# Splitting rounds spread over seven attention tiles, mixing sums on VectorE, another order at changes of pair, last down weights in used places

## What is computed

```python
h = layernorm(x) * (1 + ca) + sa
x = x + ga * attn(h)                 # sigma(q) @ memories / norms, mixed over 4 banks, @ Wo.T
h = layernorm(x) * (1 + cb) + sb
g = silu(h @ w_gate) * (h @ w_up)    # 512 -> 2048
x = x + gb * (sparsify_2to4(g) @ w_down)
```

## Time and profile before

| | us |
|---|---|
| median of 3 runs | 1488.85 |
| lowest, highest | 1488.25, 1491.37 |
| the profiled execution | 1491.06 |
| its span, first to last instruction | 1489.3 |
| PE busy | 1368.1 (92%) |
| DVE busy | 927.5 (62%) |
| ACT busy | 575.2 (39%) |
| POOL busy | 848.5 (57%) |
| mean granted clock of PE | 0.962 |

### The profile page before, as it was taken

How to read it: one execution, slowest core, us unless ns; L and a number is a source line. 1 busy time by engine, 2 the same in 40 slices (tenths; PEclk the granted TensorE clock), 3 DMA queues, 4 the chain that set the end, 5 groups by cost and what they waited for, 6 DMA issues and landing times.

```text
span 1489.3 us, 18667 instructions
## 1 busy us (share of the span) xinstructions
PE 1368.1 (92%) x6578; PEld 1105.1 (74%) x6578; DVE 927.5 (62%) x1408; ACT 575.2 (39%) x973; POOL 848.5 (57%) x856
## 2 busy tenths in 40 slices
PE   8999999999988999977988998989999899999976
PEld 4688788777767887756766777867788787888865
DVE  6677777766154555435665565756666567666776
ACT  5467667764322322232332342223343232333231
POOL 1877787787565565547885772266553235342224
PEclk9999999999999999988999999999999999999998
DMA  6656566658794756786867787848576583664512
GB/s 234 199 159 203 183 183 198 212 167 320 240 296 138 240 146 203 249 302 211 281 208 238 233 260 271 317 133 287 191 232 219 186 310 121 235 223 147 182 48 80
DMA packets 198285, 315.95 MB, mean 212 GB/s; under 512 B 12468, under 2 KB 146100, under 8 KB 183740
## 3 DMA queue, kind: packets, MB, share of 16 engines
q1 hardware_dynamic: 173868, 150.31, 32.3%
q0 software_dynamic: 24336, 164.64, 31.9%
HBM read 221.56 MB, written 93.34 MB: 211 GB/s over the span
## 4 chain that ended last, share of the span: by engine, by line
PE 52%; POOL 16%; DMA 10%; issue 8%; DVE 7%; ACT 6%; SPq 2%; POOLq 0%; DVEq 0%; ACTq 0%
PE bank L1561 17%; PE bank L1562 16%; PE bank L1563 16%; POOL hs_lo L694 3%; POOL mix L603 2%; DMA mix<-in_w_gu_dram 2%; DMA mix<-in_w_down_dram 2%; POOL banks_r L646 2%; POOL h_lo L572 2%; DMA mix<-h2T_scratch 1%; SPq L405 1%; POOL y L702 1%; PE bank L1632 1%; PE bank L1570 1%; DVE banks_r L1276 1%
## 5 line engine op out<-in xcount | busy, mean ns | idle before, releaser
L1561 PE MATMUL bank<-acts,ring 128*128 128x512 f32 x928 | 372.1, 401 | 53.7 <-ACT keep_u L984 23.1
L1562 PE MATMUL bank<-acts,ring 128*128 128x512 f32 x928 | 368.8, 397 | 0.0
L1563 PE MATMUL bank<-acts,ring 128*128 128x512 f32 x928 | 368.4, 397 | 0.0
L694 POOL TENSOR_TENSOR hs_lo<-hidden,hs_hi 128x512 fp32r<-128x512 f32 x120 | 163.7, 1380 | 245.2 <-ACT hs_hi L1006 245.2
L1561 PEld LDWEIGHTS bank<-acts,ring 128*128 128x128 f32 x928 | 179.1, 193 | 98.8 <-issue 49.8
L1561 PE MATMUL bank<-wd,hs_hi 128*128 128x512 f32 x480 | 194.5, 405 | 24.7 <-POOL hs_lo L694 17.0
L1563 PEld LDWEIGHTS bank<-acts,ring 128*128 128x128 f32 x928 | 178.9, 193 | 38.4
L1562 PEld LDWEIGHTS bank<-acts,ring 128*128 128x128 f32 x928 | 179.5, 193 | 36.9
L1562 PE MATMUL bank<-wd,hs_hi 128*128 128x512 f32 x480 | 191.2, 398 | 0.0
L1563 PE MATMUL bank<-wd,hs_lo 128*128 128x512 f32 x480 | 190.7, 397 | 0.0
L603 POOL TENSOR_TENSOR mix<-mix,mix_hi 128x512 fp32r<-128x512 f32 (+1 forms) x64 | 101.9, 1606 | 112.9 <-ACT mix_hi L866 112.4
(11 more groups left out here) (153 smaller groups left out, 2599.0 us busy)
## 6 DMA issues: line engine op xcount, KB each, us to landing
ring<-wmix_scratch POOLq DMA_DIRECT2D x48, 1024.0 KB, 7.6
ring<-wmix_scratch POOLq DMA_DIRECT2D x48, 768.0 KB, 5.2
wd<-wd_scratch POOLq DMA_DIRECT2D x16, 2048.0 KB, 9.7
acts<-amix_scratch POOLq DMA_DIRECT2D x25, 1024.0 KB, 8.3
mix<-in_w_gu_dram SPq DMA_DIRECT2D x64, 256.0 KB, 4.1
ring<-wmix_scratch POOLq DMA_DIRECT2D x32, 512.0 KB, 5.1
amix_scratch<-mix_hi SPq DMA_DIRECT2D x24, 448.0 KB, 3.8
amix_scratch<-mix SPq DMA_DIRECT2D x24, 448.0 KB, 5.0
```

What stands on the lines that cost most here:

```text
L694: nc.gpsimd.tensor_tensor(lo, slot_of(side, J * m + j), hi.bitcast(F32), ALU.subtract).then_inc(hs_lo_done, 1)
L1561: nc.tensor.matmul(out_, stat[0], mov[0], start=start, stop=False, skip_group_check=resumed)
L1562: nc.tensor.matmul(out_, stat[0], mov[1], start=False, stop=False, skip_group_check=resumed)
L1563: return nc.tensor.matmul(out_, stat[1], mov[0], start=False, stop=stop, skip_group_check=resumed)
```

## The change

It has these parts.
1. Splitting: seven rounds a tile in tiles 0 to 6, none in tile 7, instead of six in each of eight. All 16 down rounds are in the list; 49 places hold 8 "B", 32 "W" and 9 "D", the last 7 "D" rounds go to the mixing rounds. The seventh round's high part is copied at the start of the next tile.
2. Mixing (`TAKE`): units 0 to 3 of pair 0 take one "W" and one "D" instead of two "A"; units 4 to 11 one "W" and one "A"; 12 and 13 a "W" and a "D"; 14 a "D"; 15 none. Pair 1: two "W" in units 0 to 4 and 6, a "W" and an "A" in 5 and 7 to 11, two "A" in 12. Pair 2 as before, one "A" in units 2 to 9.
3. `mix_comb` moves from GpSimd to VectorE, to the end of each unit's work in `half`.
4. GpSimd: `load_down` first, then hs_low and `mix_low` by turns. ScalarE: the two first `hs_high` of a chunk move behind the second `mix_high`.
5. Unit 15's order becomes P6, P7, P1 of the next, P4, P2 of the next, P3; P5 of the next comes behind the down half. keep3 of unit 15 comes ahead of keep1. Loads of activations for pair 1 begin one unit sooner (unit 13).
6. The last down weights go into `acts` P1 and P2, loaded in unit 15 of pair 3. The last item's side 0 uses P5 and P6, side 1 `hs_hi` and `hs_lo`.

```diff
-        PER_TILE = SPLIT_RING
-        others = weight_rounds(*range(UNITS)) + down_rounds(0, 1)
+        PER_TILE = 7
+        others = weight_rounds(*range(UNITS)) + down_rounds(0, 1, 2, 3)
-        for t in range(NT):
+        for t in range(NT - 1):
-        weights_left, downs_left = weight_rounds(*range(UNITS)), down_rounds(2, 3)
+        weights_left, downs_left = weight_rounds(*range(UNITS)), others
-        TAKE = {0: [(0, 2, 0)] * 4 + [(1, 0, 1)] * 8 + [(2, 0, 0)] * 4,
-                1: [(2, 0, 0)] * 8 + [(0, 2, 0)] * 4,
+        TAKE = {0: [(1, 0, 1)] * 4 + [(1, 1, 0)] * 8 + [(1, 0, 1)] * 2 + [(0, 0, 1)],
+                1: [(2, 0, 0)] * 5 + [(1, 1, 0), (2, 0, 0)] + [(1, 1, 0)] * 5 + [(0, 2, 0)],
...
+            if m < ITEMS - 1 or side == 1:
+                return hs_hi[:, j], hs_lo[:, j]
+            return acts[:, P5, j // KH, j % KH], acts[:, P6, j // KH, j % KH]
+        def down_of(m, j):
             if m < ITEMS - 1:
+                return wd[:, 0, j], wd[:, 1, j]
+            return acts[:, P1, j // KH, j % KH], acts[:, P2, j // KH, j % KH]
...
+            if u == UNITS - 1:
+                return [(u, P6), (u, P7), (u + 1, P1), (u, P4), (u + 1, P2), (u, P3), (u + 1, P5)]
...
+                if m == ITEMS - 1:
+                    pool.wait_ge(p_done[P2], UNITS * (NP - 1))
+                    nc.gpsimd.dma_start(acts[:, P1:P2 + 1].rearrange("p a b c d -> p (a b c d)").rearrange(
+                        "p (i j d) -> p i j d", i=2, j=J), wd_dram[CHUNKS - 1].bitcast(F32R)).then_inc(wd_in, 16)
+                    return
...
-                for r in before(n):
-                    mix_low(r)
                 if m >= 0 and j == 0:
                     load_down(m)
-                if m >= 0:
-                    hs_low(m, cp, side, 2 * jj)
-                    hs_low(m, cp, side, 2 * jj + 1)
+                rounds = before(n)
+                for i in range(2):
+                    if m >= 0:
+                        hs_low(m, cp, side, 2 * jj + i)
+                    for r in rounds[i:i + 1]:
+                        mix_low(r)
                 for block_ in FINISH.get(u, ()) if p else ():
                     finish(p - 1, block_)
-                for r in AT_STEP[n]:
-                    mix_comb(r)
...
             def hs_high(m, c, side, j, first=False):
-                if m == ITEMS - 1:
-                    act.wait_ge(p_done[(P1, P5)[side]], UNITS * (NP - 1))
+                if m == ITEMS - 1 and side == 0:
+                    act.wait_ge(p_done[P5], UNITS * (NP - 1))
                 elif j == 0 and not first:
                     act.wait_ge(down_done, 2 * S * m + S * side)
...
+            def mix_comb(r):
+                e, kind, at = [mix[r % MIX_RING][:, i] for i in range(OPS + 1)], ROUNDS[r][0], 4 * COMBINED[r]
+                if kind == "D":
+                    return
+                dve.wait_ge(mix_in[r % MIX_RING], LOADED[r])
+                if kind == "W":
+                    nc.vector.tensor_tensor(e[4], e[3], e[2], ALU.add).then_inc(mix_step, 1)
...
                         hidden_b(p, u)
+                        combine(u)
                         up_of_b(p, u + 1)
                         if not (end and side):
                             gate_a(p, u + 2)
                         hidden_a(p, u + 1)
                         gate_b(p, u + 1)
                         hidden_b(p, u + 1)
+                        combine(u + 1)
...
+                if 0 < p < NP - 1:
+                    product(p, UNITS, P5)
```

More of the change, by code:

```diff
@@ L467, in _ @@
             for t in range(NT):
-                ra = PER_TILE * t
+                ra, last = PER_TILE * t, t == NT - 1
                 if t > 0:
+                    split_store_low(ra - 2)
+                    split_store_high(ra - 1)
                     split_store_low(ra - 1)
-                for r in range(ra, ra + 3):
-                    split_store_high(r)
+                if not last:
+                    for r in range(ra, ra + 3):
+                        split_store_high(r)
                 if t > 0:
                     store_x1(t - 1)
-                split_store_low(ra)
-                split_store_low(ra + 1)
+                if not last:
+                    split_store_low(ra)
+                    split_store_low(ra + 1)
                 if t > 0 and t + 2 < NT:
@@ L480, in _ @@
                     sp.dma_start(xr[place(t + 2)][:], x_t[t + 2]).then_inc(x_in[place(t + 2)], 16)
-                for r in range(ra + 3, ra + 6):
-                    split_store_high(r)
+                if not last:
+                    for r in range(ra + 3, ra + 6):
+                        split_store_high(r)
                 if t > 0:
                     store_h2(t - 1)
-                for r in range(ra + 2, ra + 5):
-                    split_store_low(r)
-            split_store_low(len(SPLITS) - 1)
+                if not last:
+                    for r in range(ra + 2, ra + 5):
+                        split_store_low(r)
             stored(sp, len(SPLITS) - 1)
@@ L652, in tile @@
                                             ALU.add).then_inc(comb_done, 1)
-                    if s == 1:
+                    if s == 1 and not last:
                         split_low(ra)
@@ L747, in pair @@
                     items_and_rounds(p, u)
+                    if last and u == UNITS - 1:
+                        load_down(ITEMS - 1)
                     for unit, o in unit_steps(u, last):
@@ L764, in _ @@
             m = ITEMS - 1
-            load_down(m)
             for side in range(SIDES):
@@ L913, in tile @@
                             ln_sqrt(t + 1, 0)
+                        if not first:
+                            split_hi(ra - 1)
+                        if not last:
                             normalize(t + 1, 0, xn1, xn1_done)
@@ L918, in tile @@
                         transposed()
-                        for r in range(ra, ra + 3):
-                            split_hi(r)
+                        if not last:
+                            for r in range(ra, ra + 3):
+                                split_hi(r)
                         if not first:
@@ L1028, in item_work, with first_splits @@
                     hs_high(mp, cp, 1, 3)
+            def first_splits(m, c):
+                if m == 0:
+                    act.wait_ge(x1_out, 16 * NT)
+                hs_high(m, c, 0, 0, first=m == 0)
+                hs_high(m, c, 0, 1)
             def plain_pair():
@@ L1829, in step @@
             def step(p, u):
-                for unit, o in unit_steps(u, p == NP - 1):
+                for unit, o in unit_steps(u, p == NP - 1)[:OPS if u < UNITS - 1 else OPS - 1]:
                     product(p, unit, o)
```

76 lines of the change are left out of this document (39 added, 37 removed).

## The result

| | before | changed |
|---|---|---|
| median, us | 1489.65 (1488.25 to 1491.37) | 1613.87 (1612.60 to 1614.95) |
| ratio | 1 | 1.0833 (1.0814 to 1.0852) |
| profiled execution: time, span, us | 1491.06, 1489.3 | 1612.79, 1611.0 |
| mean granted clock | 0.962 | 0.938 |

A forecast was written before the change was run, and what follows sets the result against it. The prediction took the kernel as bound by TensorE, with some 130 us of waits as the prize. Its terms, -106 + 54 + 70 + 6 + 3 = +27 us on the span of 1489.3, led to 1516 us, range 1458 to 1548.

The forecast's parts named there:

- Ring weights in pair 0: Pair 0: TensorE's ring waits and their clock go, as sums leave GpSimd and activation rounds leave units 0 to 3: -12.4 us.
- hs_lo in pair 0: Pair 0: waits for low halves of hidden values go, as GpSimd's new order puts them ahead of mix_low: -9.6 us.
- Change 0-1: Between pairs 0 and 1: the 10.2 us gap and 4.3 us lost in the next 102 matmuls go: -14.7 us.
- Changes 1-2 and 2-3: At these pair changes, P1 moved back one product shortens the wait for activations: -2.8 us each.
- Pair 1 and 2, all old losses gone: Pairs 1 and 2: old losses, such as keep3 and hs_lo waiting behind mixing, all go: -47.2 and -16.1 us.
- VectorE held in pairs 0 and 1: Down halves: sums waiting for late loads hold VectorE's y additions: +54 us in pair 0, +70 in pair 1.
- Landing at 8 to 10 us into the half: Odd steps: the second round's load lands then, giving TensorE gaps of 6 to 9 us plus 2.6 of clock.
- Pair 2, +6: Pair 2: one round a step, loads two steps ahead, so sums on VectorE cost 4 x 1.4 = 6 us.
- Last down weights: Kernel's end: their wait goes but the end is no shorter; four hs_low follow one by one: +3 us.
- Spread of the splits: Tiles with seven rounds instead of six: GpSimd's added mix_low falls in idle time: 0 us; without that cover 9.
- the first (loads keep up): Rival: lows and loads run near their floors, gaps stay 3 to 5.6 us, kernel faster, mid 1468; chance 0.27.
- The third, the shared ports: Rival: VectorE and GpSimd obstruct each other, a round of sums takes 2.6 us, not 1.1: 1531; chance 0.10.

The follow-up runs named there:

- e1: The changed kernel with the four sums of a mixing round back on GpSimd, last in each step's GpSimd work: 1487.68 us, 0.9984 of the kernel before.
- e14: The changed kernel with ring loads of units from the third on cut to 8 of 128 partitions: 1549.90 us, 1.0404 of the kernel before.
- e13: The changed kernel with both mix_low of a step ahead of both hs_low on GpSimd again: 1538.63 us, 1.0338 of the kernel before.
- e8: e1 with the last item's down weights and high and low halves in their old places: 1483.02 us, 0.9954 of the kernel before.
- e4: The changed kernel with every mix load from the fourth on cut to 8 of 128 partitions: 1601.46 us, 1.0761 of the kernel before.
- e2: The kernel before with only the sums moved to VectorE, at the changed kernel's places in its order: 1537.78 us, ratio 1.0312.
- e17: The changed kernel, sums on VectorE behind the third y addition, mix loads ahead of stores, old last-down-weight places, both mix_low ahead of both hs_low: 1463.83 us.

## Why the prediction was right in direction and wrong in size

The sum gave +27 us on the span and the measured difference is +122. Of the 95 us between them, 37 lie in pair 1, 29 in pair 0, 17 in pair 2, 5 in the change 0-1. Two steps of the prediction failed. One took the old waits for hs_lo and keep_u as gone, though both operands still come through mix_high and the sums (points 2 and 5). The other was the time at which the odd step's load lands, 8 to 10 us into the half (points 6 and 7). What held TensorE, VectorE's queue behind its loads, was right.

1. **Ring weights in pair 0, -12.4**: right. TensorE waits 0.2 us for the ring instead of 10.0, and the first down half starts at 433.2 instead of 445.8.
2. **hs_lo in pair 0, -9.6**: wrong, in sign. The step that failed is "the new order on GpSimd puts them ahead of mix_low". hs_low waits for ScalarE's hs_high, and that stands behind the mix_high of the step's second round, which now waits for VectorE's sums (ScalarE waited 143.5 us for them: 79.6 for L1402, 63.9 for L1409). TensorE waited some 24 us for hs_lo in pair 0, where it had waited 5.1. Being early in GpSimd's order doesn't help an operation whose operand is late; it only makes mix_low later.
3. **Change 0-1, -14.7** (its terms, 10.2 and 4.3, make 14.5): -9.9. The gap of 10.2 went, but activation loads and their clock left 4.8 us of loss in the 102 products.
4. **Changes 1-2 and 2-3, -2.8 each**: the gaps came as computed (0.8 and 2.3 to 2.5), the clock behind them cost 2.1 us, not the 1 that I gave it; pair 3's stage gained 0.5.
5. **Pair 1 and 2, all old losses gone, -47.2 and -16.1**: wrong. keep3 still stands behind mix_high and mix_high behind the sums, only on another engine: keep_u 19.8 us instead of 23.1. In pair 2, 7.8 us of keep_u stayed of 8.9, the waits for y came on top, and the stage grew by 4.1 where I had -12.9. The same holds for e1, which keeps 34.3 us of keep_u and is worth 2 us as a whole.
6. **VectorE held in pairs 0 and 1, 54 + 70**: the mechanism right, the size not. The halves of pair 0 that I priced took 31.7, 32.5, 28.6 and 30.5 us instead of 10.88, together 79.7 over, and the next one 4.7: my 54 is 30 too little. Each has a y gap of 8.7 to 9.6, at the upper end of what I gave, but also 3.3 to 7.2 of hs_lo, which I had put down as gone and then as "1 to 5 later", and half-speed clock twice. In pair 1, steps and halves are 107.8 over full speed, against my 70: y 54.2, up_b 17.5, keep_u 11.0, the rest clock.
7. **Landing at 8 to 10 us into the half**: too early. It was 16 to 21 in the four halves of pair 0, and 6.5 to 13.1 in pair 1. I took the median of weight loads, 4.0, issued by SP into other traffic; but the changed order ties the activation load to the instant at which GpSimd issues its ring loads (1.75 MB in pair 1). In pair 0 the chain also starts later. The fourth of its halves begins at 591.22:

```profile
593.39 0.29 DVE L1404 TENSOR_TENSOR mix<-mix 128x128 f32<-128x128 f32 x1 [6.99 <-DMA mix<-h2T_scratch]
596.42 0.62 ACT L1011 ACTIVATE hs_hi<-hidden 128x512 fp32r<-128x512 f32 x1
602.55 3.02 SPq L412 DMA_DIRECT2D mix<-h2T_scratch  x3
610.36 0.29 DVE L1404 TENSOR_TENSOR mix<-mix 128x128 f32<-128x128 f32 x1 [7.06 <-DMA mix<-h2T_scratch]
```

I had taken the place of the step's last hs_high from the kernel before, 2 us ahead of the half. It came 5.2 us into the half, since it stands behind mix_high, and mix_high behind the even step's sums, whose own load had only just landed. From there the loop goes through hs_low, mix_low, store and load to the next sums, 17 us after the last ones. Small ring loads take off 64 us (e14), the old order of lows 75 (e13). Together that is more than the 126 that the sums cost, so the two should overlap; no run has both.

8. **Pair 2, +6**: y took 6.6 in its four halves with rounds, as expected; the rest of the loss is point 5's and clock.
9. **Last down weights, +3**: +5.5, and 4.7 by e8; its sign and cause were right. Four hs_low one by one did follow (5.42 us from 1587.13), and the first addition came no sooner.
10. **Spread of the splits, 0**: right; products of tile 7 start at 369.1 to 373.8 in all these kernels, 370.6 in the kernel before, 371.6 in the changed one.

Of the rivals, the first (loads keep up) failed where it said it would, at gaps of over 6 us. The third, the shared ports, shows in single sums but isn't what made the kernel slow: see below. "What would show it" was fulfilled but for two points: pair 2 was to be 10 us shorter, and the gaps of down halves were released by y, but in pair 0 by hs_lo as well.

## What to carry over

Each engine works its list in order. An operation that waits for a transfer should not stand ahead of what empties a bank for the engine that bounds the kernel; moved behind the additions, the same sums on the same engine cost 101 us less. Before counting a wait as gone, follow the waiting instruction's whole queue on each engine it passes: if the operand still comes through the same chain, the wait only changes its name (34.3 us of keep_u became 48.2 of hs_lo). And price a load by what is issued beside it in the new order, not by its median in the old one.

## What the runs showed of the hardware

**Queues share by packets.** The changed kernel's part of the page on DMA queues (packets, MB, share of 16 engines' span):

```profile
q1 hardware_dynamic: 173868, 150.31, 30.0%
q0 software_dynamic: 24336, 164.64, 29.6%
```

On average SP's packets have 0.86 KB, GpSimd's 6.8 KB. The same view from 911 to 913, in the half shown above, and from 913 to 914.5:

```profile
q0 software_dynamic: 93, 0.76, 94.2%
q1 hardware_dynamic: 120, 0.06, 13.8%
...
q1 hardware_dynamic: 568, 0.28, 64.5%
q0 software_dynamic: 45, 0.24, 39.8%
```

In the first stretch the two queues send similar numbers of packets, and GpSimd's some twelve times the bytes; as its ring loads run out, SP's packets come through. A store of 448 KB by SP beside 1.75 MB by GpSimd took 9.2 us, as long as the ring loads; with those at 1/16 it took 4.0. A load of 1/16 behind that store gained little (e4). The Trainium skill has a rule for it, in "DMA: Bandwidth & Descriptors", section "Queues, rings and completion order": each engine takes turns between its queues, a packet from each. The stretch from 911 to 913 agrees, if the page's packet is the profile's, which nothing here shows. That small load and store stand in one queue would explain e4, but no run moved the load to another queue. The extreme stood in e2: a mix load issued 0.4 us behind a store of SP's, with seven activation loads of 1 MB and four ring loads from GpSimd around them, landed after 24.6 us, and one down half waited 22.65 for y.

**The shared ports.** On VectorE a sum of 128x128 took 0.27 to 0.29 us alone; beside GpSimd's operations most took much longer. VectorE, then GpSimd, in the changed kernel:

```profile
760.80 3.24 DVE L1402 TENSOR_TENSOR mix<-mix 128x128 f32<-128x128 f32 x1
...
761.37 1.29 POOL L694 TENSOR_TENSOR hs_lo<-hidden,hs_hi 128x512 fp32r<-128x512 f32 x1
762.60 1.28 POOL L595 TENSOR_TENSOR mix<-mix,mix_hi 128x512 fp32r<-128x512 f32 x1
```

The sum ends with GpSimd's second operation. 20 rows of sums took over 0.8 us, every one beside a GpSimd operation; the mean round took 1.56 us instead of 1.1, some 25 us of VectorE's time in all. How much of it lay on the path no run separates. This agrees with the rule of "SBUF — State Buffer" in the Trainium skill that the prediction named, an exclusive lock for a whole instruction, though in this row the sum began first and was held over two of GpSimd's instructions. But it didn't decide: e17 has the same 56 rounds on VectorE, at 1.54 us each, and is the fastest.

**Clock behind a gap.** Behind the gap of 10.1 us the granted clock was 0.50, the level of 1.2 GHz; the block's last 24 matmuls took 8.18 us instead of 5.44, so this gap costs 2.7 more than itself, close to the 2.6 that the prediction had from the earlier trace rows.
